# A head-pair attention pass: the order of its work where the pair changes, and where its first keys are projected

## The reference

```
h  = layernorm(x)
q  = (h @ Wq + bq)          # 1024 x 1024, 16 heads of 64
k  = (ctx @ Wk + bk)        # 6404 x 1024
v  = (ctx @ Wv + bv)
a  = softmax(where(mask, q k^T / 8, -inf))
x  = x + (a @ v) @ Wo + bo
```

## Time and profile before

| | |
|---|---|
| runs of the kernel before | 5881.00, 5881.42, 5891.56 us, median 5881.42 |
| the profiled execution | 5886.45 us, of which the span from first to last instruction is 5884.7 |
| cross attention 0, by its first key projection and its last addition to X | 259.7 to 2555.2 us |
| opening, by the first maxima unit and the first exponential | 269.4 to 411.4 us |
| PE, DVE, ACT, POOL busy over the whole span | 88%, 56%, 58%, 38% |

### The profile page before, as it was taken

The page is one execution under the profiler, slowest core; times in us unless marked ns, Lnnn a source line. Parts: engine busy times, 40 slices in busy tenths (PEclk is TensorE's granted clock), DMA queues, the critical chain, the costliest instruction groups (busy, mean ns, idle before and its releaser), DMA issues. The chain is left out here.

```text
span 5884.7 us, 67056 instructions
## 1 busy us (share of the span) xinstructions
PE 5185.2 (88%) x26382; PEld 1644.7 (28%) x26382; DVE 3321.2 (56%) x3660; ACT 3427.6 (58%) x3498; POOL 2222.3 (38%) x1111
## 2 busy tenths in 40 slices
PE   8869999999999998979999689999886788888889
PEld 3213333333333332333243311111342111111123
DVE  5677777777777775214541410000246999988713
ACT  4456565656666665721022389999224677777861
POOL 1119898989888898924634000000000000000000
PEclk8869999999999999989999799999897799999999
DMA  1000000000000000000000130000203000000010
GB/s 50 15 1 1 1 1 1 1 1 1 1 1 1 1 1 1 1 22 20 2 1 4 36 99 11 20 11 2 78 27 118 18 11 11 11 11 11 7 46 31
DMA packets 64427, 100.61 MB, mean 17 GB/s; under 512 B 9846, under 2 KB 49880, under 8 KB 62000
## 3 DMA queue, kind: packets, MB, share of 16 engines
q1 hardware_dynamic: 63906, 95.50, 4.9%
q10 hardware_dynamic: 206, 0.83, 0.0%
HBM read 70.85 MB, written 25.31 MB: 16 GB/s over the span
## 5 line engine op out<-in xcount | busy, mean ns | idle before, releaser
L2459 ACT ACTIVATE Pr<-ps,key_bias 128x1024 f32<-128x1024 f32 x816 | 868.1, 1110 | 768.0 <-PE ps L2344 767.8
L2547 DVE TENSOR_REDUCE red<-ps 128x2 f32<-128x1024 f32 (+1 forms) x767 | 902.7, 1177 | 398.7 <-PE ps L2331 398.6
L2624 POOL TENSOR_TENSOR Ps<-Ps,Pr 128x1024 f32<-128x1024 f32 x400 | 946.3, 2366 | 212.8 <-ACT Pr L2459 211.0
L2633 POOL TENSOR_TENSOR Ps<-Ps,Pr 128x1024 f32<-128x1024 f32 x400 | 947.0, 2368 | 5.8 <-ACT Pr L2459 5.6
L3251 DVE TENSOR_REDUCE red<-ps 128x1 f32<-128x512 f32 (+3 forms) x1024 | 877.2, 907 | 94.5 <-PE ps L3124 74.9
L3207 ACT ACTIVATE Pr<-ps 128x1024 f32<-128x1024 f32 x816 | 786.1, 1021 | 226.7 <-PE ps L3134 225.8
L2344 PE MATMUL ps<-Q,Kr 64*128 64x512 f32 x3264 | 809.5, 610 | 45.6 <-DVE ps L2312 25.3
L2361 PE MATMUL ps<-Pr,Vc 128*64 128x512 f32 x3264 | 791.5, 606 | 0.0
L2312 DVE CAST ps<-seeds 128x1024 f32<-128x1024 bf16 x529 | 634.9, 1221 | 176.7 <-ACT Pr L2459 167.0
L3381 ACT ACTIVATE Pr<-ps 128x2048 f32<-128x2048 f32 x467 | 726.2, 2035 | 1.6 <-PE ps L3344 1.6
L3124 PE MATMUL ps<-Kp,Q 52*128 52x512 bf16 (+1 forms) x1664 | 442.0, 411 | 172.1 <-DVE red L3251 125.9
(11 more groups left out here) (574 smaller groups left out, 5156.1 us busy)
## 6 DMA issues: line engine op xcount, KB each, us to landing
L_dram_K<-parts SPq DMA_DIRECT2D x26, 384.0 KB, 2.9
Kp<-L_dram_K SPq DMA_DIRECT2D x14, 624.0 KB
L_dram_K<-parts SPq DMA_DIRECT2D x26, 256.0 KB, 2.9
wB<-L_ffn_shares SPq DMA_DIRECT2D x1, 6144.0 KB
w<-L_ffn_experts_w_dram SPq DMA_DIRECT2D x24, 256.0 KB
Kp<-L_dram_K SPq DMA_DIRECT2D x14, 416.0 KB
wB<-L_ffn_shares SPq DMA_DIRECT2D x1, 3584.0 KB, 13.0
ctx<-ctx_dram SPq DMA_DIRECT2D x13, 256.0 KB, 7.7
```

Source lines behind the costliest of these rows:

```text
L2459: nc.scalar.activation(Pr[:, t % 4, half].rearrange("p a n -> p (a n)"), ps[:, 2 * half:2 * half + 2, :].rearrange("p a n -> p (a n)"), AC ...
L2547: nc.vector.tensor_reduce(red[:, g // C % 2, q, :, g % C], ps[:, maxima_bank(g, s, steps, q):maxima_bank(g, s, steps, q) + 2, 0:ctx.keys_i ...
L2624: nc.gpsimd.tensor_tensor(into, into, src, ALU.add).then_inc(*summed0.up())
L2633: nc.gpsimd.tensor_tensor(into, into, src, ALU.add).then_inc(*summed1.up())
```

## The change

- **Maxima at a change of pair.** A turn `leads` when it holds the last chunk of a pair (c11; six turns, g = 25, 38, ... 90). Its eight units now lie in its first three steps (2, 3, 3), and its fourth step takes the first two units of the next chunk. The turn after it (c12, three steps) has 2, 2, 2 units in place of 2, 3, 3. DVE does `neg` at the end of step 2 of the leading turn and `mz` at the end of its step 3; both stood after the whole turn.
- **Queries** of a pair are projected one turn earlier (c10, step 1).
- **Reciprocals, product and output** of a pair: the eight reciprocals stood in consecutive steps, c0 step 2 to c2 step 1; they now stand in every second step, c0 step 2 to c4 step 0. The product `Ur*over` moves from c2 step 1 to c4 step 2, the output from c2 step 2 to c5 step 1. The last pair keeps its order.
- **Opening.** For g < 14 keys are projected into bank 6. The first projection stands ahead of the wait for the norm, and the bias matmuls go to bank 7 behind the queries. The queries of pair 1 stand in turn 11 and no longer in turn 12.

```diff
+    def leads(g):
+        return LAG <= g < N - 1 and g % C == C - 1
+
     def maxima_at(g, s, steps):
-        return range(8 * s // steps, 8 * (s + 1) // steps) if 0 <= g < N else range(0)
+        if not 0 <= g < N:
+            return []
+        if leads(g):
+            return [[(g, 0), (g, 1)], [(g, 2), (g, 3), (g, 4)], [(g, 5), (g, 6), (g, 7)], [(g + 1, 0), (g + 1, 1)]][s]
+        own = [(g, q) for q in range(2 if leads(g - 1) else 0, 8)]
+        return own[len(own) * s // steps:len(own) * (s + 1) // steps]
...
-        return [(item, p) for item, p in ((item, pair_for(g, s, turn, step)) for item, turn, step in
-                (("queries", -1, 1), ("first_rows", C, 1), ("second_rows", C, 2), ("sums", LAG + C, 1), ("output", LAG + C + 2, 2))) if p is not None]
+        return [(item, p) for item, p in (("queries", query_pair(g, s)), ("first_rows", pair_for(g, s, C, 1)), ("second_rows", pair_for(g, s, C, 2)),
+                ("sums", pair_for(g, s, LAG + C, 1)), ("output", weighted_pair(g, s, LAG + C + 5, 1, LAG + C + 2, 2))) if p is not None]
...
+    def query_pair(g, s):
+        return 0 if (g, s) == (-1, 1) else pair_for(g, s, -2, 1)
+
+    def weighted_pair(g, s, turn, step, last_turn, last_step):
+        if (g, s) == (last_turn + C * (P - 1), last_step):
+            return P - 1
+        p = pair_for(g, s, turn, step)
+        return None if p == P - 1 else p
...
+    def key_bank(i):
+        return 6 if i < LAG else 4
...
         def keys(i, j):
-            take_banks(4, *([key_copied.at(i + 1)] if i < N else []), *([value_set.at(j + 1)] if 0 <= j < N else []))
+            if i < LAG:
+                take_banks(6, key_copied.at(i + 1))
...
         for g, j, steps in turns():
             for s in range(steps):
+                if (g, s) == (-1, 1):
+                    nc.tensor.wait_ge(*normed[0])
+                    nc.tensor.wait_ge(*normed[1])
+                if (g, s) == (-1, 2):
+                    constant()
...
+                if leads(g) and s == 2:
+                    largest_of_pair(g // C)
+                if leads(g) and s == 3:
+                    spread_of_pair(g // C)
                 for n in range(8):
-                    p = pair_for(g, s, LAG + C + (n + 2) // 4, (n + 2) % 4)
+                    p = weighted_pair(g, s, LAG + C + (2 * n + 2) // 4, (2 * n + 2) % 4, LAG + C + (n + 2) // 4, (n + 2) % 4)
                     if p is not None:
                         inverse(p, n)
-                p = pair_for(g, s, LAG + C + 2, 1)
+                p = weighted_pair(g, s, LAG + C + 4, 2, LAG + C + 2, 1)
```

More of the change, by code:

```diff
@@ L2321, in take_banks, with maxima @@
             taken[b] = when_free
-        def maxima(i, s, steps, q):
-            b = maxima_bank(i, s, steps, q)
+        def maxima(g, s, steps, unit):
+            (i, q), b = unit, maxima_bank(g, s, steps, unit)
             take_banks(b, taken_off(i, q))
@@ L2406, in output, with constant @@
             mm.then_inc(*out_mm.up())
-        nc.tensor.wait_ge(*zeroed.at(1))
-        for t in range(P):
-            mm = nc.tensor.matmul(ps[:, 0, 0:1], lhsT=wo[:, t, :], rhs=bv[:, t:t + 1], start=t == 0, stop=t == P - 1)
-        mm.then_inc(*constant_mm.up())
-        nc.tensor.wait_ge(*constant_set.at(1))
-        nc.tensor.wait_ge(*normed[0])
-        nc.tensor.wait_ge(*normed[1])
+        def constant():
+            nc.tensor.wait_ge(*zeroed.at(1))
+            for t in range(P):
+                mm = nc.tensor.matmul(ps[:, 7, 0:1], lhsT=wo[:, t, :], rhs=bv[:, t:t + 1], start=t == 0, stop=t == P - 1)
+            mm.then_inc(*constant_mm.up())
         for g, j, steps in turns():
             for s in range(steps):
+                if (g, s) == (-1, 1):
[3 more added lines that the diff above has]
+                    constant()
                 t = KT * (j // C) + TPC * (j % C) + s
-                items = list(maxima_at(g, s, steps))
+                items = maxima_at(g, s, steps)
                 others = others_at(g, s)
@@ L2536, in inverse, with largest @@
             nc.vector.reciprocal(over[:, sl], over[:, sl]).then_inc(*inverse_step.up())
-        def largest(g, s, steps, q):
-            if g < C and q in by_act:
-                waiting.append((g, q))
+        def largest(g, s, steps, unit):
+            i, q = unit
+            if i < C and q in by_act:
+                waiting.append((i, q))
                 if len(waiting) > 2:
@@ L2543, in largest, with largest_of_pair, spread_of_pair @@
                 return
-            nc.vector.wait_ge(*maxima_mm.at(8 * g + q + 1))
-            if g >= 2 * C and g % C == 0 and q == 0:
-                nc.vector.wait_ge(*rows_step.at(2 * (g // C) - 3))
-            nc.vector.tensor_reduce(red[:, g // C % 2, q, :, g % C], ps[:, maxima_bank(g, s, steps, q):maxima_bank(g, s, steps, q) + 2, 0:ctx.keys_in(g % C)], AX, ALU.max).then_inc(*reduced.up())
+            nc.vector.wait_ge(*maxima_mm.at(8 * i + q + 1))
+            if i >= 2 * C and i % C == 0 and q == 0:
+                nc.vector.wait_ge(*rows_step.at(2 * (i // C) - 3))
+            b = maxima_bank(g, s, steps, unit)
+            nc.vector.tensor_reduce(red[:, i // C % 2, q, :, i % C], ps[:, b:b + 2, 0:ctx.keys_in(i % C)], AX, ALU.max).then_inc(*reduced.up())
+        def largest_of_pair(p):
+            nc.vector.wait_ge(*taken_off(C * p + C - 1, max(q for q in range(8) if p or q not in by_act)))
+            if p:
+                nc.vector.wait_ge(*rows_step.at(2 * p))
+            nc.vector.tensor_reduce(neg[:], red[:, p % 2], AX, ALU.max, negate=True).then_inc(*rows_step.up())
+        def spread_of_pair(p):
+            nc.vector.wait_ge(*rows_step.at(2 * p + 1))
+            if p:
+                nc.vector.wait_ge(*rows_mm.at(2 * p))
+            nc.vector.tensor_copy(mz[:].rearrange("p q a n -> p (q a) n"), neg[:].rearrange("p q a -> p (q a)").unsqueeze(2).to_broadcast([128, 16, 128])).then_inc(*rows_step.up())
         for g, j, steps in turns():
@@ L2592, in dve @@
                     nc.vector.tensor_tensor(Ur[:], Ur[:], over[:], ALU.mult).then_inc(*inverse_step.up())
-            if 0 <= g < N and g % C == C - 1:
+            if 0 <= g < N and g % C == C - 1 and not leads(g):
                 p = g // C
@@ L2596, in dve @@
                     fold(*waiting.pop(0))
-                nc.vector.wait_ge(*taken_off(g, max(q for q in range(8) if p or q not in by_act)))
                 if p == 0:
```

48 lines of the change are left out of this document (26 added, 22 removed).

## The result

The kernel after takes 5850.09 us (median of five runs, 5834.45 to 5852.99), the kernel before, run beside it, 5883.17 (5881.00 to 5891.56). The ratio is 0.9939, its 95% interval 0.9928 to 0.9950: 33 us faster, outside the band of 5869.7 to 5893.2 that the prediction calls the same, and on the other side of before from the forecast of 5901. The profiled execution took 5850.3 us, of which the span is 5848.6.

What follows compares the result with a forecast made beforehand. PE was taken to set the pace, with DVE's margin 0.35 us a step. Opening -22, six changes +43 and last pair -2 gave +19 on 5886.45, 5905.5; the median, 5.0 lower, gave 5901 us, range 5838 to 5950.

Steps and rivals of the forecast that it cites:

- the one on the product: c4 step 2 of each change: `Ur*over` is passed over by POOL's adds, +7.9 us, with the clock's fall +10.3.
- Rival A: Product gets in at the first add boundary, a 0.1 us shift decides; change -2.4 us, in all 5843; chance 0.25.
- the opening: Layer norm's last matmul to the opening's end: earlier start, keys in bank 6, moved queries; -22 us, ends -12 to -30.
- the six changes: Turns around each change of pair: +7.1 us in sum, six times +43.
- the last pair: POOL sets the pace there and the product waits anyway; its gap of 9.80 splits in two smaller ones, -2 us.
- c10: Queries come into this turn: +3.2 us by the output as analogue, +0.5 for the two steps after, +3.7.
- `mz`: First step of c12: enters in a POOL idle gap of 0.3 us, 1.7 us late, 2.9 us long; keys wait 2.4.
- c12: Two units a step remove a reduce from both rows steps: 22.04 us becomes 19.7, -2.3 a change.
- The start: First projection follows the layer norm's last matmul, queries start at 258.1 in place of 263.04: -4.9 us.
- The eleven turns: Opening turns with keys in bank 6 each go like the quickest, 7.2 us: -15.1, between -7.5 and -22.9.
- Behind the eleven turns: Queries of pair 1 stop a full-width turn instead of one of 260 keys, with the second projection: -2 us, 0 to -4.
- the sign: Whole kernel slower than before: chance 0.58, against 0.32 for faster and 0.10 for the same.

Runs made afterwards that it cites:

- kernel 10: Changed kernel with POOL memsets of 0.74 us ahead of chosen adds, making longer unbroken chains before the product in changes 1 to 6; 5876.86 us in one run.
- kernel 3: Changed kernel with the product `Ur*over` moved ahead of DVE's copy into PSUM in changes 2 to 6; 5859.59 us, ratio 0.9967 to before.
- kernel 6: Changed kernel with POOL memsets of growing length ahead of its first add of c4 step 2 in the six changes; 5851.04 us in one run.
- kernel 8: Changed kernel with POOL memsets one tile earlier, ahead of the first add of c4 step 1, in the six changes; 5859.99 us in one run.
- kernel 9: Changed kernel: DVE waits behind the product (changes 1-3), longer POOL memsets (changes 4-6), DVE memsets behind the last product and `mz`; 5864.18 us in one run.
- Kernel 4: Changed kernel with POOL waiting for `mz` in leading turns and the last maxima turn, and for the product in the last pair; 5813.72 us, ratio 0.9890.
- experiment 5: Changed kernel with the opening's start as before (bias matmuls, wait for both norm halves, then keys), keys still in bank 6; 5843.03 us, ratio 0.9926.
- kernel 1: Changed kernel with the old order at changes of pair and pair 1's queries back in turn 12, only the opening new; 5853.47 us, ratio 0.9949.
- kernel 2: Changed kernel with the old start and old key bank, only the changes of pair new; 5884.27 us, ratio 1.0008.

## Why the prediction was wrong

**The step that failed** is the one on the product, +10.3 us at each of six changes. It took the earlier trace rows, two cases, for POOL's order of service ("a DVE instruction that is already waiting is passed over as long as the next add is ready"). What these two have in common and the six have not is that POOL had worked without a pause for 30.1 and 34.7 us. In c4 it had paused 0.28 us right before the add in flight, and 1.36 us some 5 us before that, and the product cost 1.30 us and the turn 20.64. The price itself was right: where kernel 10 made the wait in c4, the turn grew by 9.2 to 9.6 us, and the forecast had 9.5 between the two cases. And the text had named the point on which it would be wrong ("if POOL's order of service differs from what two cases show"); the chance of it, 0.25, was too low for two cases against a closer third, the `mz` of the earlier trace rows.

A rule stood against that step. The Trainium skill, "SBUF — State Buffer", section "Who interferes with whom", has the shared port as a lock that is held for one instruction. In the 23 products of kernels 3, 6, 8 and 9 in steady pairs and in after's six the trace agrees: DVE waited to the end of one add, 0.14 us before its recorded end. At 29.5 us and more it agrees for two `mz` at 30.1 and fails for all the others of the table, which waited 7 to 12 us. I let two rows overrule the rule everywhere; they overruled it only where they stood.

**Rival A** (5843) comes closest to 5850, though not by its reason: no shift of 0.1 us decides, as kernel 3 shows. Nor were its parts right: for the opening, the six changes and the last pair it had -22, -14 and -2, and the trace has -32, -3 and +2, and -5 and +2 in unchanged code ahead and behind. That its sum is so close is luck.

**The changes, turn by turn.** c10 +3.7 as said; c11 20.73 (20.7); `mz` 2.89 (2.9), let in at the end of the tile's second add, where POOL has a pause of 0.17 us (0.3), and PE's wait for the reduce behind it 2.48 (2.4); c1 and c2 20.22 (20.4); c3 +1.0 (+1.1); c5 22.89 (22.8). So the margin of 0.35 us in DVE's step and the output as the analogue for the queries hold. c0 stayed at 22.73 (-0.4 said). c12 is 21.79 and not 19.7 in five of six: behind the wait the granted clock falls, 0.92 over the turn, and where it does not the turn is 20.24. Why it does not in the one is not shown. The forecast had charged the clock to the product and to the held `mz`, not to a `mz` of 2.9 us. Kernel 4 shows the whole of it: without that wait c12 is 18.56. In sum a change came to -0.5 us, where the forecast without the product's price had -2.4.

**The opening**, -32 in after and -27 to -32 by the nine traces, against -22, was right in that both parts gain, and mis-sized in two of its three terms. Its own far ends, 4.9, 22.9 and 4, add up to -31.8 and not to the -30 that it gave.

The start was -4.9. The second key copy comes 9.6 us sooner, 6.4 by the early start and 3.1 by bank 6 (experiment 5). The queries start 4.70 us after the norm's last matmul, where before had 10.59 and the forecast 5.65, and their matmuls take 1.91 us in place of 3.78, at a clock of 0.82 over that stage.

The eleven turns were -15.1 and are -18.9 in after, -15.6 to -18.1 in the eight others. I had taken the quickest turn, 7.24 at half the clock, as the floor of all. It was not even the quickest of before. Before has one opening turn of 6.12 us, at a granted clock of 0.89:

```profile
309.73:315.85 6.12, 3.83 (x16) 0.82 (x14) 5.74 (x7) 5.82 (x8) 0.00 (x0) 0.89 0.00 0
```

In after five of the eleven take 6.1 to 6.7, at a higher clock. DVE's 6.49 for such a turn is no floor either (5.68 in the turn of 6.07). At 7.2 us each the eleven would have taken 79.2, and they took 75.3: what was missed is the clock, which rose in some of them.

Behind the eleven turns 4.8 us more went in after, for -2. But the eight others with this code took 27.65 to 29.46 there, and after 26.57. The gain is 1.9 to 4.8 us with 2.2 in the middle, so this term had its size. That it comes from the queries of pair 1 is not shown: kernel 1, which has them in the old turn, takes 29.20 there.

**The last pair** was +1.8 for -2. Its product waits for POOL's next pause in both places: it lasts 8.4 us in the old one and 13.5 in the new one.

The range of 5838 to 5950 held the result; the sign did not.

## What to carry to other kernels

Where DVE and POOL exclude each other, look how long POOL has worked without a pause, not how near a boundary DVE comes. In these traces, up to 28.3 us of such work, `mz` and the product waited at most for the add in flight; from 29.5 us on they mostly waited until POOL had nothing to do. If POOL has slack, let it wait for the DVE instruction by a semaphore; here such waits in three kinds of places gave some 30 to 40 us. A price seen in two places belongs to what these two have in common, and before it is charged six times, one asks whether the six have it too. And where several kernels share a stretch of code, compare that stretch over all their traces before a difference of 5 us is put down to a change.

## What the runs showed of the hardware

- A waiting DVE instruction started its work 0.14 us before the recorded end of POOL's add, in every case in which it got in, and POOL's next add was recorded as about 1 us longer (3.33 in place of 2.35 us, for a product of 1.22). This holds for the product, with two inputs in SBUF, and for `mz`, a cast with one. The `mz` of before in the six changes came 0.10 to 0.11 us before that end, so after this point, and was not delayed.
- Between 28.3 and 30.7 us of POOL's work without a pause the outcome turns. At 30.1 it differed from kernel to kernel, with the same time without a pause and the same distance to the end of the add in flight to within 0.03 us: 11.0 us or 1.8 for `mz`, and some 10 us in the whole. Nor does it go by the release of POOL's next add: `mz` got in where that came 0.088 and 0.109 us after the start of the add in flight (kernels 2 and 5), and was passed over at 0.088 (kernel 3) and 0.120 (kernel 9). What in the chip counts stays open: no run tells a time since the last pause from a time since DVE or POOL last took the port anew, and of the pauses between the 0.06 us between two memsets, which end nothing, and 0.7 us it is not shown which end the count.
- A request once passed over was not served at later boundaries either. At two of these boundaries at the last change POOL's next add had been released over 1 us after the one in flight began. It got in only when POOL had nothing left, 7 to 12 us later.
- A pure memset between two adds does not count as a pause, but a DVE instruction gets in while it runs (2.03 us in kernel 10).
